# Graph layer on one Trainium2 core: one-hots of two counted groups in one instruction, gathered groups placed by due times, tail in eight row pieces

## The reference

```
msg   = x[src] + edge                       # 53125 x 128
neigh = segment_sum(msg, dst)               # 3125 x 128
rst   = (1 + eps) * x + neigh
h     = rst @ W1 + b1                       # 3125 x 256
h     = relu(batchnorm over nodes(h) * gamma + beta)
out   = layernorm(x + h @ W2 + b2)          # 3125 x 128
```

## Time and profile before

| | |
|---|---|
| median of 3 runs | 280.74 us (280.03 to 281.6) |
| the profiled execution | 281.48 us, span 279.7 us |
| TensorE busy, 2211 products | 244.9 us (88%) |
| VectorE busy | 208.4 us (75%) |
| ScalarE busy | 131.7 us (47%) |
| GpSimd busy | 181.2 us (65%) |
| granted TensorE clock, mean over the span | 0.964 of full speed |

### The profile page before, as it was taken

One profiled execution on the slowest core, in us unless ns is written; L12 is line 12 of the kernel. 1 busy time (PEld: TensorE's weight loads), 2 busy tenths in 40 slices (PEclk: granted clock), 3 DMA queues, 4 the chain that ended last, 5 costly groups with the idle time before them and its releaser, 6 DMA issues.

```text
span 279.7 us, 7102 instructions
## 1 busy us (share of the span) xinstructions
PE 244.9 (88%) x2211; PEld 200.6 (72%) x2211; DVE 208.4 (75%) x916; ACT 131.7 (47%) x236; POOL 181.2 (65%) x117
## 2 busy tenths in 40 slices
PE   1567989999998889988899999999999859999970
PEld 1456768899987677766788888777878648844870
DVE  3888997788998778778489887876867861178990
ACT  0327864455555535545255544444443302086494
POOL 2078888888888888888888888888888920000000
PEclk9999999999999999999599999999999968999995
DMA  5955766687888777788488888776665200000033
GB/s 165 285 172 108 147 145 137 156 191 197 189 195 185 178 164 171 181 179 183 96 172 192 174 195 171 167 179 145 150 126 105 53 2 0 2 0 1 2 114 116
DMA packets 49535, 38.39 MB, mean 137 GB/s; under 512 B 5083, under 2 KB 48523, under 8 KB 49497
## 3 DMA queue, kind: packets, MB, share of 16 engines
q1 hardware_dynamic: 32829, 30.62, 38.2%
q0 software_dynamic: 14976, 6.82, 20.4%
q10 hardware_dynamic: 1692, 0.48, 0.9%
HBM read 36.31 MB, written 1.60 MB: 136 GB/s over the span
## 4 chain that ended last, share of the span: by engine, by line
PE 46%; DMA 16%; issue 14%; POOL 9%; DVE 7%; ACT 4%; SPq 2%; DVEq 0%; ACTq 0%; POOLq 0%
PE ps L641 18%; PE ps L649 12%; DMA egat<-in_x_dram,srci 9%; POOL egat L402 9%; DMA egat<-in_edge_attr_dram 7%; PE ps L679 5%; PE ps L673 4%; PE ps L595 4%; ACT big L527 3%; PE ps L665 2%; SPq L321 1%; DVE big L1033 1%; DVE big L1035 1%; PE ps L670 1%; DVE hit_l L904 1%
## 5 line engine op out<-in xcount | busy, mean ns | idle before, releaser
L402 POOL DMA_INDIRECT egat<-in_x_dram,srci x104 | 172.2, 1656 | 44.0 <-issue 29.2
L488 ACT ACTIVATE big<-ps 128x500 f32 x156 | 95.1, 610 | 119.8 <-PE ps L679 91.6
L641 PE MATMUL ps<-big,xp 128*128 128x114 f16 (+8 forms) x675 | 116.9, 280 | 0.2 <-issue 0.2
L649 PEld LDWEIGHTS ps<-hit_c,ebuf 128*128 128x128 f32 x624 | 101.8, 194 | 16.6 <-DVE aggT L983 6.1
L649 PE MATMUL ps<-hit_c,ebuf 128*128 128x20 f32 x624 | 95.1, 230 | 9.1 <-DVE aggT L983 5.0
L641 PEld LDWEIGHTS ps<-big,xp 128*128 128x128 bf16 x675 | 63.0, 110 | 14.6 <-issue 1.1
L983 DVE TENSOR_TENSOR aggT<-aggT,ps 128x20 f32 x208 | 35.8, 172 | 49.8 <-PE ps L649 39.7
L910 DVE TENSOR_TENSOR hit_k<-iota_k,key 128x400 f16<-128x400 f16 x156 | 56.1, 359 | 0.0
L904 DVE TENSOR_TENSOR hit_l<-iota_k,lo 128x256 f16<-128x256 f16 x156 | 52.1, 334 | 1.7 <-issue 1.6
L679 PE MATMUL ps<-hit_k,hit_l 128*128 128x400 f16 x156 | 52.3, 335 | 0.0
L908 DVE TENSOR_TENSOR hit_k<-iota_k,key 128x300 f16<-128x300 f16 x156 | 48.2, 309 | 0.0
(11 more groups left out here) (101 smaller groups left out, 165.5 us busy)
## 6 DMA issues: line engine op xcount, KB each, us to landing
ebuf<-in_edge_attr_dram SPq DMA_DIRECT2D x78, 256.0 KB
egat<-in_edge_attr_dram SPq DMA_DIRECT2D x51, 128.0 KB
egat<-in_x_dram,srci POOLq DMA_INDIRECT x104
out_dram<-big SPq DMA_DIRECT2D x6, 256.0 KB
w_sb<-in_L_gnn_W_dram ACTq DMA_DIRECT2D x2, 128.0 KB, 6.8
rows<-in_dst_dram SPq DMA_DIRECT2D x1, 192.0 KB
rows<-in_src_dram ACTq DMA_DIRECT2D x1, 192.0 KB
egat<-in_edge_attr_dram SPq DMA_DIRECT2D x1, 66.0 KB
```

The costliest lines, as they stand in the source:

```text
L402: return nc.gpsimd.indirect_dma_start(to, None, x[:, :], bass.IndirectOffsetOnAxis(ap=ix, axis=0), compute_op=op)
L488: nc.scalar.activation(cnt[:, :, bass.ds(lows[m % LOADS], WIN)], ps[:, m % BANKS_C, 0:KEYS].rearrange("p (t n) -> p t n", n=WIN), ACT.Copy ...
L641: last = nc.tensor.matmul(ps[:, ACC + f % 2, 0:SIZES[f]], xp[:, t, n, :], cnt[:, t, STARTS[f]:STARTS[f] + SIZES[f]], start=(u == 0), stop= ...
L649: last = nc.tensor.matmul(ps[:, SUMS + w % BANKS_S, 0:WIN], rows_v[:, j * D:(j + 1) * D], hits_v, start=(j == 0), stop=(j == ROWS - 1))
```

## The change

- `hits_k(m)` is called for even m alone and makes the one-hots of groups m and m+1 by three instructions of twice the size. The ring has 8 places and not 6, and VectorE works 4 groups ahead and not 3.
- The window order comes from `arrange()`, a small planner in which every window has a cost in cycles and gathered group n comes due at 27000 + 9360 n. Run by hand with the sizes of this case, it puts the gathered groups in windows 7, 10, 14, 18, 22, 26, 29, 33, 37, 40, 44, 48, 51, 55, 59, 62, 66, 70, 73, 77, 81, 85, 88, 92, 95, 99, 103, 106, 110, 113, 117, 121, 124, 128, 131, 135, 138, 142, 145, 149, 152, 155, 159, 162, 166, 169, 173, 176, 178, 181, 184 and 207, and READY is 13, 29, 52, 86, 129, 173, 198, 206, 208.
- Parts 1 and 2 of x are no longer copied: TensorE loads them as weights right from the upper halves of xN and of a full-size remainder xr. ScalarE's copies (L496, L498) go. GpSimd's addition of b2 overwrites xN, so it now waits for the last product of block 8.
- The tail's layernorm has eight pieces (4, 4, 4, 4, 4, 2, 2 and 1 tiles), with a shift of one piece made before the moments of the next; VectorE scales piece 6 itself; ScalarE takes half 1 of the ReLU for the last two blocks.

```diff
-RING_K = 6
-AHEAD = 3
+RING_K = 8
+AHEAD = 4
+SUM = 670
+COUNT = 770
+KEPT = 810
+HITS = 2400
+TURN = 1680
+GAP = 14
+GATHER = 9360
+GATHER_FIRST = 27000
+ACT_FROM = 5
...
-    def in_window(w):
-        return (w + 1) * NG // G > w * NG // G
+    def share(ready, w):
+        for f in range(F - 1):
+            if ready[f] <= w < ready[f + 1]:
+                n, i = ready[f + 1] - ready[f], w - ready[f]
+                return f, UNITS * i // n, UNITS * (i + 1) // n
+        return 0, 0, 0
+    def arrange():
+        order = [(w + 1) * NG // G > w * NG // G for w in range(G)]
+        for _ in range(ROUNDS):
+            ready = spans([w for w in range(G) if not order[w]])
+            now, m, n, order = 0, 0, 0, []
+            for w in range(G):
+                gathered = n < NG - 1 and w < G - 1 and (m == GC or now >= GATHER_FIRST + n * GATHER)
+                gathered = gathered or w == G - 1
+                f, u0, u1 = share(ready, w)
+                own = SUM if gathered else max(SUM + COUNT + KEPT * (m < KEEP), HITS)
+                now += own + (u1 - u0) * (SIZES[f] + GAP) + TURN * (X_RATE * w < NT)
+                order.append(gathered)
+                m, n = m + (not gathered), n + gathered
...
-                pool.wait_ge(x_first_made, NB)
+                pool.wait_ge(block_multiplied, F)
...
-                        nc.scalar.activation(xp[:, t0:t1, 0, :], upper(xN[:, t0:t1, :]), ACT.Copy)
...
-                        nc.scalar.activation(xp[:, t0:t1, 1, :], upper(xr[:, b % 2, 0:t1 - t0, :]),
...
+                if b >= ACT_FROM:
+                    hb = hT[:, 1, b * BANK:b * BANK + width(b)]
+                    nc.scalar.activation(hb, hb, ACT.Relu, scale=scl[:, 1:2], bias=sft[:, 1:2])
...
-                        last = nc.tensor.matmul(ps[:, ACC + f % 2, 0:SIZES[f]], xp[:, t, n, :],
+                        part_v = x3[:, t, :] if n == 2 else upper((xN, xr)[n][:, t:t + 1, :])[:, 0, :]
+                        last = nc.tensor.matmul(ps[:, ACC + f % 2, 0:SIZES[f]], part_v,
...
-                        dve.wait_ge(counts_made, m - RING_K + 2)
+                        dve.wait_ge(counts_made, m - RING_K + 3)
...
-                    nc.vector.tensor_tensor(pairs(hit_k[:, r, 0:KEYS_A]), pairs(iota_k[:, 0:KEYS_A]),
-                                            key[:, 2 * m:2 * m + 1, :].to_broadcast([P, KEYS_A // 2, 2]), ALU.is_equal)
+                    nc.vector.tensor_tensor(hit_k[:, r:r + 2, 0:KEYS_A].rearrange("p g (n two) -> p g n two", two=2),
+                                            pairs(iota_k[:, 0:KEYS_A]).unsqueeze(1).to_broadcast([P, 2, KEYS_A // 2, 2]),
+                                            keys[:, :, 0, :].unsqueeze(2).to_broadcast([P, 2, KEYS_A // 2, 2]), ALU.is_equal)
...
-                        if m + AHEAD < GC:
+                        if m % 2 == 0 and m + AHEAD < GC:
                             hits_k(m + AHEAD)
...
-            for b in range(NB):
+            for b in range(ACT_FROM):
                 r = rl[:, b % 2, 0:width(b)]
...
+            for a in range(len(ROW_PIECES)):
+                stats(a)
+                if a > 0:
+                    shifts(a - 1)
+                moments(a)
```

More of the change, by code:

```diff
@@ L82, in gnn_layer, with spans @@
     KEYS = NT * WIN
-    def in_window(w):
-        return (w + 1) * NG // G > w * NG // G
-    C_AT = [w for w in range(G) if not in_window(w)]
-    G_AT = [w for w in range(G) if in_window(w)]
+    UNITS = NT * PARTS
+    def spans(c_at):
+        return [c_at[g - 1] + SETTLE for g in ENDS[:-1]] + [G]
+    def share(ready, w):
[17 more added lines that the diff above has]
+                m, n = m + (not gathered), n + gathered
+            short = NG - sum(order)
+            at = [w for w in range(G) if not order[w]]
+            for w in at[len(at) - short:] if short > 0 else []:
+                order[w] = True
+        return order
+    IN_WINDOW = arrange()
+    C_AT = [w for w in range(G) if not IN_WINDOW[w]]
+    G_AT = [w for w in range(G) if IN_WINDOW[w]]
     C_OF = {w: m for m, w in enumerate(C_AT)}
     G_OF = {w: n for n, w in enumerate(G_AT)}
-    READY = [C_AT[g - 1] + SETTLE for g in ENDS[:-1]] + [G]
-    UNITS = NT * PARTS
+    READY = spans(C_AT)
     def units(w):
[L95 to L99, removed]
+        return share(READY, w)
+    ROW_PIECES = [(t, t + 4) for t in range(0, NT - 5, 4)] + [(NT - 5, NT - 3), (NT - 3, NT - 1), (NT - 1, NT)]
     EARLY = STARTS[-1] // BANK
@@ L370, in _ @@
                         chunk(C_OF[w] // CHUNK + CHUNKS)
-            for b in range(NB):
-                t0, t1 = pieces(b)
+            for t0, t1 in ROW_PIECES[:6]:
                 sp.wait_ge(rows_normalised, t1)
[L375 to L379, removed]
+                sp.dma_start(out_v[:, t0:t1, :], oN[:, t0:t1, :]).then_inc(rows_written, 16)
+            t0, t1 = ROW_PIECES[6]
+            sp.wait_ge(late_rows_normalised, t1 - t0)
+            sp.dma_start(out_v[:, t0:t1, :], oN[:, t0:t1, :]).then_inc(rows_written, 16)
+            sp.wait_ge(rows_normalised, NT - 2)
+            sp.dma_start(out[(NT - 1) * P:N, :], oN[0:NL, NT - 1, :]).then_inc(rows_written, 16)
+            sp.wait_ge(rows_written, 16 * len(ROW_PIECES))
         @block.gpsimd
@@ new lines, in hits_k @@
+                    nc.vector.tensor_tensor(hit_k[:, r:r + 2, KEYS_A:KEYS_A + KEYS_B].rearrange("p g (n two) -> p g n two", two=2),
+                                            pairs(iota_k[:, FROM_B:FROM_B + KEYS_B]).unsqueeze(1).to_broadcast(
+                                                [P, 2, KEYS_B // 2, 2]),
+                                            keys[:, :, 1, :].unsqueeze(2).to_broadcast([P, 2, KEYS_B // 2, 2]),
+                                            ALU.is_equal).then_inc(key_hits_made, 2)
@@ L927, in rest @@
                     t0, t1 = pieces(b)
[L928 to L931, removed]
+                    nc.vector.tensor_tensor(xr[:, t0:t1, :], xN[:, t0:t1, :], upper(xN[:, t0:t1, :]),
                                             ALU.subtract).then_inc(x_rest_made, 1)
@@ L1035, in _ @@
                 nc.vector.tensor_scalar(hb, r, 0.0, None, ALU.max).then_inc(relu_half1_made, 1)
[L1037 to L1056, removed]
@@ new lines, in stats, with moments @@
+            def stats(a):
+                t0, t1 = ROW_PIECES[a]
+                r = rows_of(t1 - 1)
+                dve.wait_ge(rows_made, a + 1)
+                for t in range(t0, t1):
+                    k = (t - t0) * D
+                    nc.vector.bn_stats(lst[0:r, t, :], ps[0:r, (a + 4) % 8, k:k + D]).then_inc(row_stats_made, 1)
+            def moments(a):
+                t0, t1 = ROW_PIECES[a]
+                r = rows_of(t1 - 1)
+                for t in range(t0, t1):
+                    dve.wait_ge(row_stats_made, t + 1)
+                    nc.vector.bn_aggr(lag[0:r, t, :], lst[0:r, t, :]).then_inc(row_moments_made, 1)
@@ new lines, in _ @@
+            for a in range(len(ROW_PIECES)):
[3 more added lines that the diff above has]
+                moments(a)
+            t0, t1 = ROW_PIECES[6]
+            dve.wait_ge(row_shifts_made, 7)
+            for t in range(t0, t1):
+                k = (t - t0) * D
+                nc.vector.tensor_scalar(oN[:, t, :], ps[:, 2, k:k + D], lrs[:, t:t + 1], lnb[:, t:t + 1],
+                                        ALU.mult, ALU.add).then_inc(late_rows_normalised, 1)
```

104 lines of the change are left out of this document (56 added, 48 removed).

## The result

| | median us | runs |
|---|---|---|
| kernel before, same chip | 280.38 | 4 (279.57 to 281.6) |
| changed kernel | 292.68 | 4 (291.58 to 293.54) |

The ratio is 1.0433, with a 95% interval of 1.0379 to 1.0486: slower, by 12.3 us. The profiled execution of the changed kernel took 291.58 us, span 289.8.

The account below looks back on a forecast made before the run. GpSimd's gather issues, without slack from 15 to 219 us, were taken to set the pace. 281.48 + 13.3 (window order) + 2.5 (port) + 0.3 (weights) - 0.8 (tail) = 296.8 us profiled, 296.0 median; range 292 to 300.

Parts of the forecast that it names:

- port term: GpSimd's gather issues wait longer for merged VectorE one-hots: +2.5 us, between bounds of 0 and +6.
- Group 50 decides: Gathered group 50, moved from window 203 to 184, still lands at about 217.5 us; windows end 13.3 us later.
- Work behind it: TensorE's work from window 184 to the end of window 207, after the last early gather: 35.6 us.
- Idle time before it: TensorE, otherwise at window 184 by 197.5 us, idles 20 us over gathered windows from about group 12 on.
- The standstill's 6.6 us: Beside GpSimd's addition at 218 us, TensorE's 3.7 us stop and half clock after it; saving counted in the window term.
- Weights from upper halves: Products of blocks 7 and 8 slow down with weight steps of 4 bytes: +0.3 us, lower bound 0.
- Rival C: VectorE's statistics in the first layer are locked out by GpSimd's moved addition: 300.5 us, chance 0.08.
- Tail: Earlier ReLU on VectorE and smaller last pieces after the first layer: -0.8 us, between bounds of 0 and -1.4.
- Pairs: One-hots merged two groups at a time save 16 us of VectorE work, off the path: worth 0.
- Rivals A: Gathers keep their floor rate of 1.85 us a step, so group 50 lands 8.4 us sooner: 285.1 us, chance 0.12.
- B (faster): GpSimd is no limit, with issues every 1.81 us; about 275 us if every 1.75; chance 0.07.
- D: Merged one-hots on VectorE lose their 16-bit rate, 1 ns an element, not 0.5: about 302 us, chance 0.03.

Follow-up runs that it names:

- experiment 7: Changed kernel with the planner's floor for a counted window at 1700 cycles, not 2400, and one-hots made one group at a time: 265.32 us, ratio 0.9497.
- experiment 2: Kernel before with only the gathered windows' places changed to the new list: 301.54 us, ratio 1.0819.
- experiment 4: Kernel before with the new list of places and GpSimd's addition of b2 moved behind block 8: 293.24 us, ratio 1.0446.
- experiment 3: Kernel before with only GpSimd's addition of b2 moved behind the last product of block 8: 274.46 us, ratio 0.9812.
- experiment 8: Changed kernel with the planner's floor at 1700 cycles, not 2400, and all of the tail as in the kernel before: 263.45 us, ratio 0.9427.
- experiment 6: Changed kernel with the planner's floor for a counted window at 2000 cycles, not 2400: 276.96 us, ratio 0.9844.

## Why the prediction was right

It said 296.0 us and slower, with 292 to 300 as the forecast's own range; measured were 292.68. The large term held: the last early gather decides where the windows end. Some smaller terms did not, and three signs came out short: waits for gathers of 20.1 us (25 to 35 forecast), the last issue at 215.0 (217 to 221), the first layer at 253.9 (257 to 260). Against the 296.8 us for an execution like the profiled one, 5.2 us are missing in the profiled 291.58, about 2.9 of the landing, 2.5 of the port term and 0.3 of the weights, less 0.4 of the tail.

- *Group 50 decides.* Predicted landing 217.5 us, found 214.6. Two things make the 2.9 us: the issue began 2.2 us sooner, and the landing took 3.3 us and not 3.9. The 2.2 us come from the start of GpSimd's list: its third issue begins at 19.41 and not at 22.06 (experiment 7 has the rows), while from there to group 50 the steps are as long as before (1.939 and 1.934 us). The 3.8 and 5.4 us of the earlier trace rows were both a little long for this end of the loop, where few other transfers run.
- *Work behind it.* Predicted 35.6 us; window 184 to the end of window 207 took from 214.6 to 250.2, 35.6 us. The sum from the costs of single windows and the measured end of the kernel before was good to 0.1 us.
- *Idle time before it.* Predicted 20 us more than before. Window 184 came 13.6 us later, with 3.5 us less work by the forecast's own sum, so 17.1 us are to be found (20 less the earlier landing). TensorE's waits for gathers rose by 12.2. Half clock up to there, 10.2 us against 6.8, is up to 1.7 more. Some 3 us are not accounted for. The 18.4 us of weight loads under "issue" are no further part: of the 27.4 us in the loop in which no product runs, 26.7 are without a weight load too, so the two stand still together.
- *The standstill's 6.6 us* were counted inside the 35.6, and experiments 2 and 4 show 8 to 10 us for it (4.9 of it a wait), experiment 3 alone 4.2 by the medians, with an interval that holds 6.6.
- *The port term*, +2.5, is the step that failed. From the third issue to group 50 the changed kernel took 191.9 us and the one before 191.5, so it measured 0.4. At the same places (experiment 4) the issues with pairs are longer by 0.024 us each, some 2.3 us in all, and the second issue, which the forecast had left out, is 2.8 us shorter. Set against each other they leave 0.4 us sooner at group 50's second gather (211.33 and 211.71). I had drawn the term from single long issues beside VectorE's one-hots. The Trainium skill (SBUF — State Buffer, Who interferes with whom) infers that descriptor making doesn't wait for such an instruction. Two of the four pairs of means in experiment 7, equal to 0.005 us, agree with it; the issues of 2.8 to 5.5 us, beside an unbroken run of VectorE's one-hots (last section), speak against it. These runs don't decide it.
- *Weights from upper halves*, +0.3: 0. Block 8 takes 3.63 us for 75 products with steps of four bytes as with two.
- *The moved addition* is hidden under the first layer, and the statistics beside it keep their length (after, timeline):

```profile
257.25 0.69 DVE L1059 BATCH_NORM_STATS2 big<-big 128x6 f32<-128x512 f32 x1 [0.16 <-ACT big L537]
```

  Rival C is out. By the Trainium skill (SBUF — State Buffer, Who interferes with whom) a VectorE instruction with at most one SBUF input doesn't contend with GpSimd, outside certain fast modes; this row agrees, at 0.69 us inside the addition's 254.25 to 261.23.
- *Tail*, -0.8: from the first layer's start to the end of the span 36.3 us before and 35.9 after, and experiment 8 can't tell the two apart. The rows' scaling in fact ends 0.8 us later, counted from there; smaller last transfers give it back.
- *Pairs* were costed at 0 for the path, and net that is what they gave. VectorE's busy time fell by 20.7 us, 7.7 of it from GpSimd's addition no longer holding a one-hot; that leaves 13 of the 16 us forecast. Merged they last 0.42, 0.47 and 0.57 us, against 0.41, 0.46 and 0.56 forecast. That they also bring GpSimd's early issues forward was not foreseen. My later belief that they would show once the gathers were out of the way got no support.

Rivals A (285.1) and B (faster) needed gathers at 1.85 or 1.81 us a step; they went at about 1.94 as before. D is out by the durations. The prediction's "whoever starts first holds the port for its whole length", for which it named the 7.95 us row, is not what that row shows; see the last section.

## What to carry to other kernels

Where a queue at its limit feeds another engine, what counts is how much of the consumer's work lies behind the last item that it has to wait for: find that item's landing, add the work behind it, and compare with the end. Check by the waits which item that is; in experiment 6 it was not the one assumed. An order made by a planner is only as good as its prices: here lowering the floor from 1.0 to 0.7 us, for a window that costs 0.59 beside its block work, moved the time by 28 us. Price such a model from start-to-start times in the trace, and check its total against the span.

## What the runs showed of the hardware

- A GpSimd addition with two SBUF operands of 3200 elements held a two-operand VectorE one-hot for 7.9 us (0.28 alone), twice, in two kernels; seven VectorE statistics with one SBUF operand beside the same addition kept their 0.69 us. The addition itself took 6.98 us there and 7.55 beside the one-hot. By the records the one-hot that was held had begun first, 0.24 us before the addition (218.06 and 218.30, and the earlier trace rows) and 0.23 in experiment 2, so the first to start was the one held; spans on GpSimd are rough, and this stays open.
- One gather issue near the start takes 2.8 to 5.5 us, and not 1.6, in twelve of fourteen profiles. It lies over an unbroken run of VectorE instructions, mostly one-hots, and ends 0.7 us after that run does in all twelve: in the kernel before the run ends at 21.06 and the issue at 21.75. Later runs as dense hold no issue so long (at most 2.3 us), so what decides is open.
- The lower clock (1.2 GHz) came at 35.0 to 37.2 us in nine of fourteen profiles that are nearly alike there. A wait of TensorE of 1.4 to 2.1 us stands before it in seven of them, but one profile had such a wait and kept the clock, and two had the low clock behind waits of at most 0.8 us. What decides, these runs don't show.
- Weights of bf16 read in steps of four bytes load as fast as packed ones (0.107 and 0.108 us against 0.110 in the mean), and a product of 110 columns takes 0.048 us with either.
